# Tokens sorted by their pair of chosen experts, through HBM, in place of all eight experts for every token

## The chip, the cores and the metric

The kernel runs on one core of one Trainium2 chip. The metric is the device time of one execution in microseconds (us); less is better. Work is issued to TensorE (PE; its weight loads are shown apart as PEld), VectorE (DVE), ScalarE (ACT), GpSimd (POOL) and SyncE (SP), each of which runs its own instructions strictly in order; semaphores tie them together. SPq in a row is SP's queue, which only issues DMAs.

## The reference, cut to what matters

`x` is 32 images of 64 channels and 32x32 places, that is 32,768 tokens of 64 features. Three layers follow each other, each added to its input: a gated convolution of 1x1 kernels, a linear attention with its own small two-layer network, and the layer that the change touches, a mixture of 8 experts:

```python
logits = xf @ gate_w + gate_b
probs = jax.nn.softmax(logits, axis=-1)
top2_vals, top2_idx = jax.lax.top_k(probs, 2)
cw = jnp.zeros((N, Ee), dtype=xf.dtype).at[jnp.arange(N)[:, None], top2_idx].add(top2_vals)

def step(acc, params):
    w1, bb1, w2, bb2, we = params
    h = jax.nn.gelu(xf @ w1 + bb1, approximate=False)
    y = h @ w2 + bb2
    return (acc + we[:, None] * y, None)
out, _ = jax.lax.scan(step, jnp.zeros_like(xf), (W1, b1, W2, b2, cw.T))
```

D is 64, the hidden width 128, E is 8. `cw` is zero for the six experts that a token did not choose, so only two of the eight terms count. `xf` is the layer-normed token (mean 0 over its 64 features). Everything is float32.

## The kernel before, in words

The 32 images are taken in pairs (64 channels of two images fill the 128 partitions), two pairs at a time: `GROUPS` = 8 groups of `G` = 2 slots, a slot being 128 x 1024 (`T`) values, worked on in halves of `CH` = 512 columns. One group is 4,096 tokens.

**Dense work** of a group is a chain of small stages (a PE matmul, an ACT or DVE pass over its result, the next matmul): `channel_stats` to `conv_out` (the convolution), `centre_1` to `features_1` (a layer norm), `query` to `message` (the attention), then three layer norms of the form `variance_k`, `rstd_k`, `spread_k`, `norm_k` with `hidden_0`, `hidden_1`, `hidden_out` and `centre_4` between them. The last norm leaves the experts' input in `XF`. Then the **router** (`gates` to `gate_rows`): logits, softmax and the two largest on DVE, and the 8 weights of each token, transposed by PE (L830) and copied by DVE (L1343).

**Expert work** before: the router's rows go to HBM (`gates_hbm`, L524) and come back spread over the partitions as `CWB` (L533). A group has `US` = 32 units, one for each slot, expert and half. A unit is `first_layer` (L847: 2 matmuls of 64 rows x 128 columns of weights with 512 columns of data, one for each image of the pair, in two halves of the array's rows), `gelu` on ACT (L992, 128 x 1024), `second_layer` (L861: 2 matmuls in two halves of its columns), `combine` on DVE (L1355: add the bias, multiply by the token's weight for this expert) and `add_up` on POOL (L1044: into the sum `XB`). PE writes a float32 matmul as two records, so 2 matmuls are shown as x4.

**Order.** Every engine's program is written out from one table, `SCHEDULE`: in a turn, the dense stages of group `a` stand in a fixed order, and between them stand the steps of the experts of groups `b` and `c` (the earlier ones): letters for PE, counts for ACT and DVE. From the entry `first_unit` on they belong to group a-1, ahead of it to what is left of group a-2. `OPENING` is a table of its own for the start, in which group 0's dense work runs with group 1's convolution beside it, before any expert. The last group's experts have nothing beside them; they use more buffers then (`last_group`, `FREE`), so that PE runs two units ahead.

SP issues every DMA, in the program's order: the loads of `x` (L515), the router's rows out and back, and the stores of the result (`store`, L550).

## Time and profile before

| | |
|---|---|
| median of 3 runs | 1174.67 us (1172.91 to 1174.70) |
| span of the profiled execution, first to last instruction | 1171.7 us |
| PE busy | 1058.5 us, 90% of the span |
| DVE, ACT, POOL busy | 740.2, 641.8, 361.7 us |
| HBM read, written | 78.12 MB, 9.44 MB |
| instructions recorded | 16,823 |

The profiled execution's own time is its span and a few us around it: the runs' median lies 3.0 us over that span. Read from the table that PE is what is busy nearly all the time and that every other engine has a third of its time or more free. "Busy" is the union of an engine's records, so matmuls that overlap count once. The span falls into an opening, six repeats of one period, and an end; the windows below are cut there, at the starts of the router's logits (L815).

### The profile page before, as it was taken

The page shows a single profiled execution, that of the slowest core. Times are in us where ns is not written, and L with a number is a line of the kernel's source. Part 1 is how long each engine was busy: PE and PEld are TensorE (multiplying, and loading weights), DVE is VectorE, ACT ScalarE, POOL GpSimd, SP SyncE. Part 2 cuts the span into 40 slices and gives each one's busy share as a digit, 9 for nine tenths or more (in the row PEclk, how much of TensorE's full clock was granted, in tenths as well). Part 3 has the DMA queues.
Part 4 walks back from the last instruction along what each step waited for, and adds up shares of the span by engine and source line. Part 5 has one row for each costly group of instructions (what it writes and reads, how often), then busy time and mean ns, then how long its engine had stood idle before and what let it go on. Part 6 is the DMA issues. An engine that isn't in the chain of part 4 may idle for free.

```text
span 1171.7 us, 16823 instructions
## 1 busy us (share of the span) xinstructions
PE 1058.5 (90%) x6646; PEld 442.3 (38%) x6646; DVE 740.2 (63%) x1529; ACT 641.8 (55%) x866; POOL 361.7 (31%) x280
## 2 busy tenths in 40 slices
PE   4798589979999899988999899998999989998898
PEld 1453244323533245332453235432453324532232
DVE  5744745686647875587664966468764886556344
ACT  3345355654566556664556546556556555665454
POOL 0000031333323333333232333133332342324465
PEclk9989889999999999999999999999999999999999
DMA  5000086007700284005810068000850039200760
GB/s 157 6 1 1 1 179 149 3 22 173 169 1 19 54 189 104 1 19 112 185 50 1 19 149 198 1 19 19 194 134 1 18 69 201 42 1 19 179 145 23
DMA packets 15597, 88.62 MB, mean 76 GB/s; under 512 B 3488, under 2 KB 6816, under 8 KB 11424
## 3 DMA queue, kind: packets, MB, share of 16 engines
q1 hardware_dynamic: 15520, 87.57, 32.3%
q8 instruction: 52, 0.85, 0.3%
q14 instruction: 25, 0.20, 0.1%
HBM read 78.12 MB, written 9.44 MB: 75 GB/s over the span
## 4 chain that ended last, share of the span: by engine, by line
PE 74%; DVE 12%; ACT 9%; issue 3%; DMA 1%; DVEq 0%; POOL 0%; POOLq 0%; SPq 0%
PE HP L847 15%; PE HP L861 14%; ACT H L992 5%; PE R L646 5%; PE R L621 4%; PE R L610 4%; PE R L699 3%; PE R L717 2%; PE R L708 2%; PE R L786 2%; PE R L795 2%; PE R L788 2%; PE R L861 2%; PE R L675 2%; DVE TM L1355 2%
## 5 line engine op out<-in xcount | busy, mean ns | idle before, releaser
L1044 POOL TENSOR_TENSOR XB<-TM,XB 128x512 f32<-128x512 f32 x254 | 323.0, 1286 | 658.5 <-DVE TM L1355 658.5
L992 ACT ACTIVATE H<-HP,W 128x1024 f32<-128x1024 f32 x224 | 243.0, 1116 | 205.7 <-PE HP L847 205.1
L1355 DVE SCALAR_TENSOR_TENSOR TM<-HP,B2S,CWB 128x512 f32<-128x512 f32 x224 | 163.2, 742 | 207.1 <-PE HP L861 196.3
L847 PE MATMUL HP<-XF,W1E 64*128 64x512 f32 x1024 | 269.9, 630 | 19.3 <-DVE TM L1355 18.5
L861 PE MATMUL HP<-H,W 128*64 128x512 f32 x896 | 233.1, 616 | 18.0 <-ACT H L992 18.0
L847 PEld LDWEIGHTS HP<-XF,W1E 64*128 64x128 f32 x1024 | 84.1, 187 | 143.9 <-DVE TM L1355 71.0
L861 PEld LDWEIGHTS HP<-H,W 128*64 128x64 f32 x896 | 48.5, 135 | 171.2 <-ACT H L992 116.3
L1156 DVE SCALAR_TENSOR_TENSOR BIG<-R,T 128x512 f32<-128x512 f32 x112 | 69.5, 681 | 20.9 <-PE R L610 20.8
L930 ACT ACTIVATE T<-R 128x512 f32<-128x512 f32 x96 | 57.4, 598 | 39.8 <-PE R L646 31.4
L958 ACT ACTIVATE T<-R,MINUS 128x512 f32<-128x512 f32 x64 | 41.4, 688 | 27.3 <-PE R L708 24.4
L1243 DVE SCALAR_TENSOR_TENSOR BIG<-T,R 128x512 f32<-128x512 f32 x64 | 41.8, 684 | 21.6 <-ACT T L958 21.6
L610 PE MATMUL R<-IM,REP 32*128 32x512 f32 x336 | 50.2, 482 | 5.1 <-ACT T L918 2.3
L621 PE MATMUL R<-BIG,W 128*64 128x512 f32 x224 | 53.0, 617 | 1.9 <-DVE BIG L1156 1.9
L975 ACT ACTIVATE BIG<-R,BH 128x512 f32<-128x512 f32 x64 | 40.5, 683 | 21.7 <-PE R L788 21.7
L1035 POOL TENSOR_TENSOR XB<-XN,X 128x1024 f32<-128x1024 f32 x14 | 33.2, 2396 | 54.9 <-ACT XN L953 54.9
L992 ACT ACTIVATE BIG<-HP,W 128x1024 f32<-128x1024 f32 x32 | 33.9, 1110 | 26.0 <-PE HP L847 26.0
L1355 DVE SCALAR_TENSOR_TENSOR TM<-R,B2S,CWB 128x512 f32<-128x512 f32 x32 | 24.0, 751 | 37.8 <-PE R L861 35.1
L924 ACT ACTIVATE T<-R,W 128x512 f32<-128x512 f32 x28 | 19.2, 687 | 45.5 <-PE R L621 45.5
L1163 DVE TENSOR_TENSOR X<-X,T 128x512 f32<-128x512 f32 x28 | 21.6, 773 | 32.4 <-ACT T L924 32.4
L1218 DVE SCALAR_TENSOR_TENSOR T<-R,T 128x512 f32<-128x512 f32 x64 | 40.4, 682 | 1.9 <-PE R L675 1.7
L918 ACT ACTIVATE T<-R 128x512 f32<-128x512 f32 x56 | 29.1, 602 | 21.4 <-PE R L610 21.3
L610 PEld LDWEIGHTS R<-IM,REP 32*128 32x128 f32 x336 | 21.7, 202 | 48.1 <-issue 19.6
(179 smaller groups left out, 1411.3 us busy)
## 6 DMA issues: line engine op xcount, KB each, us to landing
CWB<-gates_hbm SPq DMA_DIRECT2D x32, 1536.0 KB, 20.4
CWB<-gates_hbm SPq DMA_DIRECT2D x32, 512.0 KB, 6.6
out<-XB SPq DMA_DIRECT2D x15, 512.0 KB, 3.0
X<-x SPq DMA_DIRECT2D x14, 512.0 KB, 3.8
XF<-x SPq DMA_DIRECT2D x2, 512.0 KB, 6.1
gates_hbm<-RT SPq DMA_DIRECT2D x16, 64.0 KB, 1.6
W<-wpack SPq DMA_DIRECT2D x1, 968.0 KB, 4.9
W1E<-w1e SPq DMA_DIRECT2D x1, 512.0 KB, 7.4
```

The source lines that it names most:

```text
L610: last = mm(Ra[s][:, half(c)], REP[rows, n, :], IM[rows, s, part, :], start=(part == 0), stop=(part == 1))
L621: last = mm(Ra[s][img(k), half(c)], w("ow")[:, C * h:C * h + C], BIGa[:, s, 2 * k + h, half(c)], start=(h == 0), stop=(h == 1))
L646: return mm(R[s][:, half(c)], weights, src[:, s, half(c)], start=True, stop=True)
L847: last = mm(HP[u % BATCH][:, half(k)], W1E[img(k), e, :], XF[img(k), 1 - par, s, half(c)], start=True, stop=True)
L861: last = mm(sums_of(b, u)[img(k), :], w("w2e")[:, C * e:C * e + C], activated(b, u)[:, k, :], start=True, stop=True)
L930: f(T2[:, s, half(c)], R[s][:, half(c)], ACT.Square).then_inc(ln_sq[s], 1)
L958: f(T1[:, s, half(c)], R[s][:, half(c)], ACT.Exp, bias=MINUS[:, :]).then_inc(qk_exp[s], 1)
L992: f(activated(b, u).rearrange("p k t -> p (k t)"), HP[u % BATCH][:, :], ACT.Gelu, bias=col(B1E + e))\
L1044: nc.gpsimd.tensor_tensor(acc, TM[:, u % BATCH, :], acc, ALU.add).then_inc(acc_done, 1)
L1156: v.scalar_tensor_tensor(out=BIGa[:, s, 2 * k + h, half(c)], in0=Ra[s][:, half(c)], scalar=1.0, in1=T2a[:, s, half(c)], op0=ALU.add, op1=A ...
L1243: v.scalar_tensor_tensor(out=dst[s][:, half(c)], in0=T1[:, s, half(c)], scalar=1.0, in1=R[s][:, half(c)], op0=ALU.min, op1=ALU.max).then_i ...
L1355: v.scalar_tensor_tensor(out=TM[:, u % BATCH, :], in0=sums_of(b, u), scalar=B2S[:, e % 2, e // 2:e // 2 + 1], in1=CWB[:, s, e, half(c)], o ...
```

## The change

Each token's pair of chosen experts is one of 28 classes (`CLS`, the pairs i<j). After the router, the group's 4,096 tokens are **sorted by class** and every class is filled up to whole blocks of 64 places (`BLK`); that takes at most 92 blocks (`BLOCKS`), 5,888 places. Each block needs only its pair's weights. What is added, for each group:

- `tokens_4` ("K", 4 steps): PE transposes the 32 tiles of tokens in 16 transposes of 128x128 (L938), ACT copies them to `XFT`, one token to a row of 64 features and two shares (the weights of its two experts).
- `classes`, `shares`, `sort_1` to `sort_3`: DVE makes a one-hot of the class, PE counts with 32 tiny matmuls (L949) and adds ranks (L960 to L963), DVE makes the place of each token (`IDX`) and the class of each block (`OF_BLOCK`).
- `scatter` (POOL): 32 indirect DMAs of 128 rows of 264 bytes to `slots_hbm`.
- 12 units (`US`) of 8 blocks (the last has 4). In a unit SP loads the places twice side by side (`unit_input`), and for each block **reads the block's class from SBUF into a register** (`value_load`) and issues a DMA of 128 KB, this pair's weights, from `pairs_hbm` (`pair_weights`). PE transposes the places ("T", `unit_features`), ACT copies them adding 1.0, PE runs the first layer ("A"): for each block 4 matmuls of 64 rows x 64 columns with 64 columns of data; ACT does gelu; the second layer ("B") has 4 matmuls of 128 rows x 64 columns with 64 columns for each two blocks; DVE multiplies by the shares and adds the pair's two results; SP writes them to `y_hbm`.
- `gather` (POOL): 32 indirect DMAs of 128 rows of 256 bytes back to token order. `final` ("F", 4 steps): PE turns them back to features with matmuls and adds the experts' second biases (`B2J` times the router's rows); DVE adds that to the sum.

The first bias is folded into the weights once, at the start (the input has mean 0, so 1.0 added to it meets a bias spread over 64 rows). There, too, `pairs_hbm` is written (28 DMAs) and `slots_hbm` filled with zeros. `CWB`, `gates_hbm`, `combine`'s bias and POOL's adding up are gone, and with them the last group's special case.

A group now passes through four turns instead of three: dense; then router, sort, scatter and the first units; then the remaining units and the gather; then `final` and `store`.

```diff
-CH_UNITS = E * NCH
-US = G * CH_UNITS
+PAIRED = [(d, i) for d in range(1, E) for i in range(E - d)]
+CLS = len(PAIRED)
+TOK = G * 2 * TB
+BLK = 64
+BLOCKS = (TOK * P + CLS * (BLK - 1)) // BLK + 1
+UB = CH // BLK
+US = -(-BLOCKS // UB)
...
 SCHEDULE = [
-    ("channel_stats", "HH", 1, 0), ("gates", "", 1, 0), ("gate_tokens", "YY", 0, 0),
...
+    ("channel_stats", "KA"), ("gates", "K"), ("gate_tokens", "TB"), ("gate_exp", ""), ("group_stats", "K"),
...
+    ("numerator.0", ""), ("numerator.1", ""), ("first_unit", ""), ("attended.0", ""), ("attended.1", "T"),
...
+            for n in range(GROUPS + 3):
+                turn(group(n), group(n - 1), group(n - 2), group(n - 3), parts)
...
+                def unit_input(u):
+
+                    n = a * US + u
+                    sp.wait_ge(scat_done, 16 * TOK * (a + 1))
+                    rows = slots_hbm[a % 2][CH * u:CH * u + P * columns(u), :].rearrange("(d p) c -> p d c", p=P)
+                    sp.dma_start(SLT[:, n % 3, 0:columns(u), 0:C], rows[:, :, 0:C]).then_inc(slt_in[n % 3], 16)
+                    sp.dma_start(SLT[:, n % 3, 0:columns(u), C:C + ROW], rows).then_inc(slt_in[n % 3], 16)
+
+                def pair_weights(g, u):
+
+                    n = g * US + u
+                    sp.wait_ge(cls_done, g + 1)
+                    for q in range(blocks_of(u)):
+                        pair = nc.sync.value_load(OF_BLOCK[0:1, g % 2, u * UB + q:u * UB + q + 1], min_val=0, max_val=CLS - 1)
+                        sp.dma_start(WB[:, n % 3, q, :],
+                                     pairs_hbm[bass.ds(pair, 1), :, :].rearrange("o p c -> p (o c)")).then_inc(wb_in[n % 4], 16)
...
+                def after(u):
+
+                    n = a * US + u
+                    sp.wait_ge(comb_read, n + 1)
+                    g, ahead = divmod(n + 3, US)
+                    if g < GROUPS:
+                        pair_weights(g, ahead)
+                        if g == a:
+                            unit_input(ahead)
+                    sp.wait_ge(yo_done, n + 1)
+                    sp.dma_start(y_hbm[a % 2][CH * u:CH * u + P * columns(u), :].rearrange("(d p) c -> p d c", p=P),
+                                 YO[:, n % 2, 0:columns(u), :]).then_inc(y_out[n % 2], 16)
...
+                def first_layer(u):
+
+                    n = a * US + u
+                    pe.wait_ge(xt_copied, n + 1)
+                    pe.wait_ge(*unit_weights(n))
+                    free("L1")
+                    for q in range(blocks_of(u)):
+                        for r in range(2):
+                            for h in range(2):
+                                last = mm(L1[img(h), CH * r + BLK * q:CH * r + BLK * q + BLK], WB[img(r), n % 3, q, img(h)],
+                                          XT[img(r), n % 2, BLK * q:BLK * q + BLK], start=True, stop=True)
...
+                def second_layer(u):
...
+                    for d in range(columns(u)):
+                        for r in range(2):
+                            for h in range(2):
+                                q = 2 * d + h
+                                last = mm(YPS[img(h), d, r, :], H[:, n % 2, r, BLK * q:BLK * q + BLK],
+                                          WB[:, n % 3, q, HID + C * r:HID + C * r + C], start=True, stop=True)
...
+                def scatter():
+
+                    pool.wait_ge(idx_done, a + 1)
+                    pool.wait_ge(tok_copied, (a + 1) * len(PIECES))
...
+                    for t in range(TOK):
+                        nc.gpsimd.indirect_dma_start(out=slots_hbm[a % 2], in_=XFT[:, t, :], in_offset=None,
+                                                     out_offset=bass.IndirectOffsetOnAxis(ap=IDX[:, a % 2, t:t + 1], axis=0))\
+                            .then_inc(scat_done, 16)
+
+                def gather():
+
+                    for k in range(2):
+                        pool.wait_ge(y_out[k], 16 * (US // 2) * (a + 1))
...
+                    v.tensor_tensor(YT[:, there, :, :], YPS[:, there, :, :],
+                                    SLT[:, n % 3, there, P:P + 2].unsqueeze(3).broadcast_to([P, columns(u), 2, C]), ALU.mult)\
+                        .then_inc(comb_read, 1)
...
+                    v.tensor_tensor(YO[:, n % 2, there, :], YT[:, there, 0, :], YT[:, there, 1, :], ALU.add).then_inc(yo_done, 1)
```

How the instructions stand now, at two places. **SP, one turn**, before (the waits are in brackets; L550 stores, L533 spreads the router's rows, L515 loads `x`, L524 writes the router's rows):

```order
L550 DMA out<-XB 128x1024 [waits acc_done]
L533 DMA CWB<-gates_hbm 64x2048 [waits comb_done]
L533 DMA CWB<-gates_hbm 64x2048
L533 DMA CWB<-gates_hbm 64x6144 x2
L515 DMA X<-x 128x1024 [waits xs_done0]
L515 DMA X<-x 128x1024 [waits xs_done1]
L550 DMA out<-XB 128x1024 [waits acc_done]
L524 DMA gates_hbm<-RT 128x128 [waits cwt_done]
L524 DMA gates_hbm<-RT 128x128
```

and SP of the change, between two units (CWB is the tensor in which all the new buffers lie; L595 and L596 are `unit_input`, L628 writes a unit's result, L603 is the read of the class with its register instructions, L604 the DMA of its weights):

```order
L595 DMA CWB<-slots_hbm 128x4x64 [waits scat_done]
L596 DMA CWB<-slots_hbm 128x4x66
L628 DMA y_hbm<-CWB 128x4x64 [waits yo_done]
L603 TENSOR_LOAD OF_BLOCK [waits cls_done,comb_read]
L603 ISA x2
L604 ISA
L604 DMA CWB<-pairs_hbm 128x256
L603 TENSOR_LOAD OF_BLOCK
```

In a period SP had 14 DMAs; it now has 92 reads of a class with 276 register instructions and 92 DMAs of weights, beside 40 others.

**PE, from the spreading of the attention's denominator (L770, now L869) to the second norm's spreading (L675, now L774)**, before:

```order
L770 MATMUL R<-BIG,SPREAD 128x256 x8
L847 MATMUL HP<-XF,W1E 128x512 x2
L646 MATMUL R<-T,WMC 128x512 x4
L861 MATMUL HP<-H,W 64x512 x2
L662 MATMUL R<-T,LINES 32x128 x16
L847 MATMUL HP<-XF,W1E 128x512 x2
L861 MATMUL HP<-H,W 64x512 x4
L675 MATMUL R<-BIG,SPAN 128x128 x16
```

and in the change (L972 "T", L985 "A", L1000 "B"):

```order
L869 MATMUL R<-BIG,SPREAD 128x256 x8
L972 MATMUL HP<-W,CWB 128x128 x4
L745 MATMUL R<-T,WMC 128x512 x4
L985 MATMUL HP<-CWB 64x64 x32
L761 MATMUL R<-T,LINES 32x128 x16
L972 MATMUL HP<-W,CWB 128x128 x4
L1000 MATMUL HP<-CWB,H 64x64 x16
L774 MATMUL R<-BIG,SPAN 128x128 x16
```

The dense matmuls and their order are the same; between them stand 32 and 16 matmuls of 64 columns where there were 2 to 4 of 512.

## Rows read from the trace of the kernel before

**Rows 1.** The page: busy time of the engines, and the chain that ended last

```profile
PE 1058.5 (90%) x6646; PEld 442.3 (38%) x6646; DVE 740.2 (63%) x1529; ACT 641.8 (55%) x866; POOL 361.7 (31%) x280
...
PE 74%; DVE 12%; ACT 9%; issue 3%; DMA 1%; DVEq 0%; POOL 0%; POOLq 0%; SPq 0%
```

**Rows 2.** Windows: from:to, length, busy of PE, PEld, DVE, ACT, POOL, clock, DMA, GB/s

```profile
0.00:137.00 137.00, 101.37 (x696) 52.26 (x696) 80.58 (x196) 54.66 (x94) 6.19 (x12) 0.96 0.12 35
137.00:234.40 97.40, 81.91 (x579) 37.92 (x578) 55.41 (x122) 52.11 (x73) 24.90 (x18) 0.93 0.45 100
...
373.10:511.80 138.70, 130.21 (x834) 54.19 (x832) 93.54 (x192) 80.34 (x109) 45.95 (x35) 1.00 0.34 78
...
1066.60:1171.70 105.10, 94.42 (x392) 27.33 (x384) 45.95 (x73) 53.29 (x51) 57.94 (x46) 0.98 0.43 99
```

**Rows 3.** One period by line: L847, L861 (PE, PEld), L1355 (DVE), L992 (ACT), L1044 (POOL)

```profile
373.10:511.80 138.70, 34.20 (x132) 10.59 (x130) 1.00 0.34 78
...
373.10:511.80 138.70, 32.99 (x128) 6.94 (x128) 1.00 0.34 78
...
373.10:511.80 138.70, 23.24 (x32) 1.00 0.34 78
...
373.10:511.80 138.70, 37.37 (x35) 1.00 0.34 78
...
373.10:511.80 138.70, 41.31 (x33) 1.00 0.34 78
```

**Rows 4.** L815, the logits, from the second group on: durations, first and last start

```profile
L815 PE MATMUL R<-XF,GWZ x112: 376/379/403, 234.5 to 1066.8; 128*32 128x256 f32 x112
```

**Rows 5.** Timeline of PE: start, length, line, shape, records [idle before]

```profile
438.66 1.09 PE L641 MATMUL R<-W,BIG 128*128 128x128 f32 x8
439.68 1.13 PE L847 MATMUL HP<-XF,W1E 64*128 64x512 f32 x4
...
447.15 1.05 PE L708 MATMUL R<-W,XN 128*128 128x128 f32 x8
448.04 0.38 PE L681 MATMUL R<-ONE 128*128 128x512 bf16 x1
...
469.64 1.08 PE L662 MATMUL R<-T,LINES 128*32 128x128 f32 x32
470.65 1.13 PE L847 MATMUL HP<-XF,W1E 64*128 64x512 f32 x4
```

**Rows 6.** SP's queue: two issues at the start; all issues of L533 (ns, min/median/max)

```profile
2.12 0.43 SPq L467 DMA_DIRECT2D BIG<-reps  x1
2.60 0.43 SPq L468 DMA_DIRECT2D BIG<-reps  x1
...
L533 SPq DMA_DIRECT2D CWB<-gates_hbm x64: 444/597/779, 151.8 to 1110.0; - x64
```

**Rows 7.** DMA: the hardware queue; issues with KB of each and us to landing

```profile
q1 hardware_dynamic: 15520, 87.57, 32.3%
...
gates_hbm<-RT SPq DMA_DIRECT2D x16, 64.0 KB, 1.6
```

**Rows 8.** Groups of instructions: busy us, mean ns of one | idle before

```profile
L1044 POOL TENSOR_TENSOR XB<-TM,XB 128x512 f32<-128x512 f32 x254 | 323.0, 1286 | 658.5 <-DVE TM L1355 658.5
...
L1035 POOL TENSOR_TENSOR XB<-XN,X 128x1024 f32<-128x1024 f32 x14 | 33.2, 2396 | 54.9 <-ACT XN L953 54.9
...
L1210 DVE TENSOR_TENSOR BIG<-R,SM 128x512 f32<-128x512 f32 x32 | 20.5, 683 | 0.2
...
L1327 DVE TENSOR_TENSOR RT<-RT 128x256 f32<-128x256 f32 x8 | 3.4, 426 | 0.3
```

**Rows 9.** Timeline of PE: the router's wait in the opening

```profile
138.71 0.44 PE L822 MATMUL HP<-W,BIG 128*128 128x128 f32 x2 [0.66 <-ACT BIG L981]
148.25 0.69 PE L830 MATMUL HP<-W,RT 128*128 128x128 f32 x2 [9.11 <-DVE RT L1333]
```

More of the change, by code:

```diff
@@ L552, in parts @@
-                return {**slotwise("features_1", next_input), "gate_rows": gate_weights,
-                        "weights_1": last_weights, "finish_0": lambda: store(0), "finish_1": lambda: store(1)}, lambda step, u: None
-            turns(parts, DVE_STEPS, apart=1)
+                        sp.wait_ge(pair_out, 16 * 4 * (E - 1))
+                        for u in range(3):
+                            pair_weights(a, u)
+                    for u in range(3):
+                        unit_input(u)
@@ new lines, in sort_3 @@
+                def sort_3():
+                    pe.wait_ge(d_done, 2 * (a + 1))
+                    for some, there in RANK_PARTS:
+                        mm(L1[:, there], BEFORE[:, :], MH[:, some, :].rearrange("p t k -> p (t k)"), start=True, stop=False)
+                        mm(L1[:, there], UNIT_ONE[0:CLS, :].broadcast_to([CLS, P]), RANKS[0:CLS, some.start * CLS:some.stop * CLS],
+                           start=False, stop=True)
+                    mm(TABLE, CLSID[0:CLS, :], OWNER[0:CLS, :], start=True, stop=True).then_inc(rank_ps, 1)
+                    last_read["L1"] = (cls_done, a + 1)
@@ L863, in second_layer @@
-                    last.then_inc(y_ps, 1)
-                def expert(step, u):
-                    if step == FIRST:
-                        if u < BATCH or not last_group(b):
-                            first_layer(u)
-                        return
-                    if last_group(b) and u % BATCH == 0:
-                        for ahead in range(u + BATCH, min(u + 2 * BATCH, US)):
-                            first_layer(ahead)
-                    second_layer(u)
+                    n = a * US + u
@@ new lines, in second_layer, with final @@
+                    last.then_inc(y_ps, 1)
+                def final(i):
+                    s, blocks, _ = tiles(i)
+                    if a == 0 and i == 0:
+                        pe.wait_ge(b_in, 16 * 2 * TB)
+                    pe.wait_ge(gath_done, 16 * TOK * (a + 1))
+                    free("XP")
+                    for k, j in enumerate(blocks):
+                        t = 2 * (s * TB + j)
+                        mm(XP[:, P * k:P * k + P], YG[:, t:t + 2, :].rearrange("p k c -> p (k c)"), w("ident"), start=(k == 0), stop=False)
+                    for k, j in enumerate(blocks):
+                        rows = img(j * NCH // TB)
+                        last = mm(XP[:, P * k:P * k + P], B2J[rows, k, :], CWR[rows, a % 3, s, :], start=False, stop=(j == blocks[-1]))
+                    last.then_inc(fin_ps, 1)
+                    last_read["XP"] = (fin_added, a * len(PIECES) + i + 1)
@@ L1054, in _ @@
+                return {**slotwise("features_1", residual), "sort_3": scatter, "gather": gather}, {}
+            turns(parts)
         @block.vector
@@ L1387, in parts @@
                     "choose_1": choose_1, "choose_2": choose_2, "gate_rows": gate_rows,
-                }, expert
-            turns(parts, DVE_STEPS)
+                    "classes": classes, "shares": shares, "sort_1": sort_1, "sort_2": sort_2, "sort_3": sort_3,
+                }, {"F": final, "B": combine}
+            turns(parts)
 def kernel(**inputs):
```

535 lines of the change are left out of this document (338 added, 197 removed), and 38 rows, old and new, of tables (OPENING, SCHEDULE).

## The prediction

> **What bounds it now.** I read the page first: PE is busy 90% of the span, and the chain that ended last is 74% PE [rows 1]. Then windows cut at the router's logits. The span is an opening of 137.0 us, a turn of 97.4, six periods, and an end of 105.1 [rows 2]; logits start at 234.5 and, six groups later, at 1066.8 [rows 4], so a period is 832.3 / 6 = 138.7 us. In it PE is busy 130.2 us at a clock of 1.00 (2.4 GHz), DVE 93.5, ACT 80.3, POOL 46.0, the DMA engines 34% [rows 2]. PE bounds it, and its idle time is 8.5 us. 34.2 + 33.0 = 67.2 us of PE's time are the experts [rows 3], the dense work is the other 63.0. The reader is to see two things: the six periods are 71% of the time, and in the end PE is still busy 94.4 of 105.1 us, since there the experts run at PE's pace.
>
> The sum goes: opening + turn + 6 periods + end, each priced anew.
>
> **The period, by PE.** Removed: 67.2 us. Added:
> - Small matmuls: 92 blocks x 4 in the first layer and 46 x 4 in the second are 552, two records each: 1,104. The nearest row is L662, where 32 records of 128 columns in quarters of the array go by in 470.65 - 469.64 = 1.01 us, 31.6 ns each [rows 5]. So 34.9 us. Bounds: below, four quadrants at once with 64 columns, half of L662's columns, 16 ns and 17 us; above, a full-width record as in L641 (1.02 us / 8 = 128 ns for 128 columns [rows 5]), halved for 64 columns, 64 ns and 71 us. I stay at L662, the only row with short records and part of the array.
> - Transposes: 46 of the units and 16 of the tokens at 128 ns: 7.9 us.
> - `final`: 32 matmuls of 128 columns as L708, (448.04 - 447.15) / 4 = 0.22 us [rows 5]: 7.1 us.
> - The sort: 32 tiny matmuls at L662's pace 1.0 us, and the rank and table matmuls, some 1,700 columns or 13 times 128, at L708's 0.22: 3.9 us in all.
>
> That is 53.8 us in place of 67.2: **PE gains 13 us a period, not the three quarters of the experts' work that the arithmetic drops**, because 552 matmuls of 64 columns cost by their number. With the 8.5 us of idle time the period by PE is 63.0 + 53.8 + 8.5 = 125.3 us.
>
> The Trainium skill (TensorE: Matmul & The Clock Gate, section "Wait — 56ns, not 53.3ns?") says that matmuls never start closer than about 25 ns however short; the 31.6 ns of the row respect that floor. At it, the 1,104 records would take 27.6 us and the period by PE would be 118.0; the row at 31.6 ns is what I use.
>
> **The period, by SP.** SP had 14 issues a period and idled; it now has 92 times a register read, three register instructions and a DMA issue, and 40 other DMAs. A plain issue takes 0.43 us and the next follows 0.05 us after it [rows 6]; L533's take 0.60. No row shows a register read. Bounds: below, the 0.05 us of a step that is not listed; above, 1.6 us, which is a whole small transfer from issue to landing [rows 7], since a read has its way there and back in common with one. I take 0.60, what the dearer plain issue L533 takes, as it is a trip without descriptors. A block is then 0.60 + 3 x 0.05 + 0.45 = 1.20 us, and a period 92 x 1.20 + 40 x 0.50 = 130.4 us. At the bounds: 80 and 222 us.
>
> The Trainium skill (DMA: Bandwidth & Descriptors, "Latency and other measured facts") gives about 600 ns as a register load's floor, and its rules warn that transfers under 64 KB are mostly overhead. A floor of 0.60 would take the cheap half of my bounds away and make a faster kernel less likely.
>
> So SP and PE lie within 5 us of each other, and PE must wait for weights where SP is late: **132 us** for the period, 6.7 less than before.
>
> **The period, other engines.** DVE loses L1355's 23.2 us [rows 3] and gains 12 x (0.68 + 0.43) = 13.3 for the products and sums [rows 8], some 3 for `final`, 13 for classes, shares and sorting: 100 us of 132, hidden but closer. ACT loses 37.4 and gains about 23. POOL loses 41.3 and gains 64 indirect DMAs. No row shows one: below is SP's 0.43, above L1035's 2.40, the longest POOL instruction; I take 1.3, L1044's 1.29 [rows 8], since both write 128 partitions from POOL: 83 us, hidden. The scatter takes 42 us between `sort_3` and the first "T", which are some 44 us apart: its cover is just enough. DMA: 78 GB/s x 138.7 us = 10.8 MB become 12.1 (weights) + 4.6 (places and results) + 2.1 (scatter, gather) + 2.1 = 20.9 MB; q1 moved 87.57 MB in 32.3% of the span, 231 GB/s [rows 7], so 90 us at that rate. Hidden, if 1 KB pieces go as fast.
>
> **Opening and turn.** Before, PE waited 9.1 us for the router in the opening [rows 9]. Group 0's sort now follows with nothing beside it: three round trips of PE and DVE, 12 us in which PE's dense work of group 1 stands behind the sort's matmuls. Then the scatter, 42 us, and only then the first "T"; the dense stages up to there cover some 25. So +29 us: 137 + 126 = 263. The tables, `pairs_hbm` and the zeros are written beside the opening, at nothing; without that cover they'd cost a few us.
>
> **The end.** Before 105.1 us. After the last logits 8 units of group 6 are left, then 12 of group 7, with no dense work beside them. PE needs some 4 us a unit; SP needs 8 x 1.20 + 3 x 0.50 = 11.1. Three units' weights are loaded ahead, so SP's pace holds for 8 + 9 = 17 units: 189 us. To that, 18 us for the first and the last of them to go through, 44 for the last gather, of which every one of 32 DMAs is on the path, 8 for `final` and the store: **259 us, 154 more than before**. What was a PE-bound end becomes an end bound by SP and by POOL.
>
> **Sum.** 263 + 6 x 132 + 259 = 1314 us of span, 142 more than 1171.7. The median of the runs is 3 us over the span: **1317 us**, 12% slower. As a formula: 263 + 6 x period + 17 x unit + 70.
>
> **Rivals.**
> - *Cheap register reads and matmuls that overlap (faster).* If a block costs SP 0.80 us (a read of 0.20), SP's period is 94 us and a unit 7.9. With small matmuls at 20 ns the period by PE is 112.5. Then 255 + 675 + 134 + 65 = 1129 span, 1132 us. The point from which it decides: the period below 117 with a block below 0.85 us. For it: PE's idle time is small, so what PE saves shows. Against it: L662 is dear though its columns are few. Both must hold, so 0.24.
> - *Both partly so (the same).* Period 118 and block 0.80: 255 + 708 + 134 + 70 = 1167 span, 1170 us. 0.04.
> - *Dear register reads.* At 1.6 us a block is 2.2: period 222, unit 19.1: 270 + 1332 + 325 + 75 = about 2000 us. At 1.0 us: 1.6, 167, 14.3: 263 + 1002 + 243 + 70 = 1578. Nothing in the trace speaks against it but L533. 0.12 for 1578 and up.
> - *Indirect DMAs dear.* At L1035's 2.4 us, POOL has 64 x 2.4 + 5 = 159 us a period, and scatter and gather are 77 us each: 298 + 954 + 189 + 105 = 1546, with 3 around it 1549 us. 0.08. The Trainium skill (SBUF — State Buffer, section "SBUF: two separate sides") says that GpSimd cannot write its DMA descriptors while DVE copies in its fast mode, which would be one way into this case; no row here shows it.
> - *DMA engines as the bound.* If 1 KB and 256 B pieces go at half of 231 GB/s, 20.9 MB take 181 us a period: 263 + 1086 + 259 = 1608. Against it: the register reads space the transfers. 0.04.
> - That it doesn't do what it says: I see no such way; the 92 blocks are computed whether full or not.
>
> **Chances and range.** The forecast, with its bounds (period 122 to 145, unit 10 to 12.5: 1235 to 1420), has 0.48. Of the middle case's 0.04, half lies within 0.2% (about what a measurement of this kernel can tell from no change) and a quarter on either side. So faster 0.25, the same 0.02, slower 0.73. The range leaves out the dear reads and the slow DMA engines, 0.16, and the fastest end of the cheap case: 1120 to 1570.
>
> **What would show it.** In the profile after, I look for: PE's busy time per period near 117 and its small records 30 ns apart; SP's queue solid with loads and issues, a block every 1.2 us; PE's longest waits at the first layer, for weights (`CWB` from `pairs_hbm`); a period of 132; DVE near 100 and POOL's 64 DMAs near 83 us; an end of some 260 us. The prediction is wrong if a block on SP takes under 0.85 us, or if scatter or gather DMAs, and not the weights, are what PE waits for.

## The result, and the profile after

The changed kernel takes **1512.7 us** (median of 4 runs, 1509.9 to 1519.6) where the one before takes 1174.7: a ratio of 1.289, 95% interval [1.285, 1.292]. It is slower, as forecast, and by 338 us, not by 142. The profiled execution took 1511.5 us, its span is 1509.7. Some kernels below have executions of two kinds, some per cent apart, the longer ones at a lower granted clock: the ratios compare the shorter ones, and the profiled executions of e5 and e6 (1406.4 and 1377.3 us) are of the longer kind.

The page of the changed kernel, busy time of the engines, the clock in 40 slices and the DMA queues (against [rows 1, 7]):

```profile
PE 1049.6 (70%) x14783; PEld 709.8 (47%) x14798; DVE 735.9 (49%) x1702; ACT 531.7 (35%) x832; POOL 543.9 (36%) x545
...
PEclk9899679969797979788989798988889895657755
...
q1 hardware_dynamic: 272400, 159.30, 40.1%
q0 software_dynamic: 16384, 17.07, 4.8%
```

PE has as much busy time as before, in a span 29% longer, and its clock, at or near full speed nearly everywhere before, swings in every period.

Windows of the changed kernel at the same places of the program as [rows 2]: opening, turn, one of the six periods, end (from:to, length, busy of PE, PEld, DVE, ACT, POOL, clock, DMA share, GB/s):

```profile
0.00:151.10 151.10, 114.49 (x726) 61.56 (x730) 82.91 (x203) 54.70 (x94) 7.68 (x19) 0.95 0.29 84
151.10:277.80 126.70, 73.43 (x974) 46.39 (x974) 60.08 (x140) 41.12 (x68) 36.01 (x34) 0.78 0.28 71
595.30:754.10 158.80, 125.62 (x1859) 85.31 (x1865) 92.39 (x214) 66.64 (x105) 67.40 (x66) 0.87 0.52 134
1230.40:1509.70 279.30, 127.76 (x2093) 107.30 (x2085) 45.85 (x100) 34.99 (x46) 92.35 (x96) 0.63 0.44 114
```

The logits (L914 now, against [rows 4]):

```profile
L914 PE MATMUL R<-XF,GWZ x112: 379/379/403, 277.8 to 1230.6; 128*32 128x256 f32 x112
```

So a period is (1230.6 - 277.8) / 6 = 158.8 us. By the parts of my sum: opening and turn 277.8 (I said 263), periods 953 (792), end 279 (259). Of the 196 us that I missed in the span, **161 lie in the periods**: each is 26.8 us longer than forecast. In one, PE is idle for 33.2 us, where I kept the 8.5 of before.

What PE waits for in that period, by line (us in total, times, longest):

```profile
PE HP L972 <- DMA CWB<-slots_hbm: 16.7, 4, 10.2
PE R L774 <- DVE BIG L1399: 3.5, 3, 1.2
PE HP L938 <- DVE XF L1411: 2.9, 2, 1.4
PE R L745 <- DVE XB L1424: 2.5, 2, 1.6
```

The largest wait is at the transposes of "T", for the **places** of a unit, not at the first layer for weights. Over the six periods it comes to 105.0 us in 21 times, 17.5 a period. SP's queue around the longest of them (start, length, issues):

```profile
685.35 8.38 SPq L604 DMA_DIRECT2D CWB<-pairs_hbm  x8
693.78 0.43 SPq L628 DMA_DIRECT2D y_hbm<-CWB  x1
695.03 8.02 SPq L604 DMA_DIRECT2D CWB<-pairs_hbm  x8
703.10 0.43 SPq L628 DMA_DIRECT2D y_hbm<-CWB  x1
703.58 0.47 SPq L595 DMA_DIRECT2D CWB<-slots_hbm  x1
```

and PE there:

```profile
706.80 1.12 PE L972 MATMUL HP<-W,CWB 128*128 128x128 f32 x4 [10.25 <-DMA CWB<-slots_hbm]
```

The places of the new group's first unit stand in line behind 16 tiles of weights, those of the second and third unit, which are not needed yet. SP is not solid: in this period it waits too.

```profile
SPq L603 <- DVE CWB L1593: 28.3, 4, 11.6
```

Those 28.3 us are waits for a free weight buffer (VectorE's L1593 is the step that ends a unit's use of it). SP works in bursts: idle, then some 9 us for a unit, with what is urgent at the end of the burst. What one block costs it (ns, min/median/max):

```profile
L603 SPq TENSOR_LOAD <-OF_BLOCK x736: 262/268/901, 183.7 to 1433.5; - x184
L603 SPq FUSED_REGOPS  x736: 152/152/188, 184.3 to 1433.8; - x184
...
L604 SPq DMA_DIRECT2D CWB<-pairs_hbm x736: 337/338/1090, 184.8 to 1434.2; - x184
```

Eight blocks take about 8.9 us with the read ahead of the first, 1.12 each.

### The profile page after: what moved, and what is told of

The parts are those of the page before. It is cut to its first block and busy times, and to the rows that moved or that the text cites. A ratio compares the mean times of both kernels' runs of the same rounds, so it can differ in the third digit from the quotient of the medians.

```text
span 1509.7 us, 38760 instructions
## 1 busy us (share of the span) xinstructions
PE 1049.6 (70%) x14783; PEld 709.8 (47%) x14798; DVE 735.9 (49%) x1702; ACT 531.7 (35%) x832; POOL 543.9 (36%) x545
## 5 line engine op out<-in xcount | busy, mean ns | idle before, releaser
L1212 POOL DMA_INDIRECT slots_hbm<-CWB,IDX x256 | 254.7, 995 | 488.4 <-DVE IDX L1579 412.8
L1223 POOL DMA_INDIRECT CWB<-y_hbm,IDX x256 | 248.7, 972 | 293.8 <-issue 198.5
L972 PE MATMUL HP<-W,CWB 128*128 128x128 f32 x368 | 76.5, 340 | 240.6 <-DMA CWB<-slots_hbm 224.7
L1593 DVE TENSOR_TENSOR CWB<-HP,CWB 128x512 f32<-128x512 f32 x96 | 63.8, 664 | 258.5 <-PE HP L1000 258.5
L1154 ACT ACTIVATE H<-HP 128x1024 f32<-128x1024 f32 x96 | 94.9, 989 | 248.7 <-PE HP L985 222.4
L972 PEld LDWEIGHTS HP<-W,CWB 128*128 128x128 f32 x368 | 48.4, 169 | 277.1 <-DMA CWB<-slots_hbm 244.3
L1000 PE MATMUL HP<-CWB,H 128*64 128x64 f32 x2944 | 130.7, 254 | 6.6 <-ACT H L1154 6.5
L1000 PEld LDWEIGHTS HP<-CWB,H 128*64 128x64 f32 x2944 | 117.0, 165 | 31.3 <-issue 19.0
L985 PE MATMUL HP<-CWB 64*64 64x64 f32 x5888 | 126.8, 244 | 5.1 <-DVE OF_BLOCK L1574 4.4
L985 PEld LDWEIGHTS HP<-CWB 64*64 64x64 f32 x5888 | 112.8, 156 | 32.1 <-issue 26.6
L1013 PE MATMUL HP<-W,CWB 128*128 128x128 f32 x256 | 47.8, 344 | 49.0 <-DMA CWB<-y_hbm,IDX 44.7
L1013 PEld LDWEIGHTS HP<-W,CWB 128*128 128x128 f32 x256 | 40.7, 242 | 59.4 <-DMA CWB<-y_hbm,IDX 44.8
```

The costliest lines, as they stand in the source:

```text
L972: last = nc.tensor.transpose(XP[:, P * d:P * d + P], SLT[:, n % 3, d, 0:P], w("ident"))
L985: last = mm(L1[img(h), CH * r + BLK * q:CH * r + BLK * q + BLK], WB[img(r), n % 3, q, img(h)], XT[img(r), n % 2, BLK * q:BLK * q + BLK], s ...
L1000: last = mm(YPS[img(h), d, r, :], H[:, n % 2, r, BLK * q:BLK * q + BLK], WB[:, n % 3, q, HID + C * r:HID + C * r + C], start=True, stop=True)
L1013: mm(XP[:, P * k:P * k + P], YG[:, t:t + 2, :].rearrange("p k c -> p (k c)"), w("ident"), start=(k == 0), stop=False)
L1154: f(H[:, n % 2, :, some], L1.rearrange("p (r t) -> p r t", r=2)[:, :, some], ACT.Gelu).then_inc(gelu_done, 1)
L1212: nc.gpsimd.indirect_dma_start(out=slots_hbm[a % 2], in_=XFT[:, t, :], in_offset=None, out_offset=bass.IndirectOffsetOnAxis(ap=IDX[:, a % ...
```

## The experiments

All kernels in one table; periods and ends are cut at the logits as above, from the profiled execution, whose mean clock stands in the last column. A row's median is that of all its runs.

| kernel | median us | ratio to before | period | end | clock |
|---|---|---|---|---|---|
| before | 1174.7 | 1 | 138.7 | 105 | 0.985 |
| the change | 1512.7 | 1.289 [1.285, 1.292] | 158.8 | 279 | 0.83 |
| e1 pairs fixed | 1392.8 | 1.184 [1.179, 1.190] | 147.5 | 229 | 0.844 |
| e4 places first | 1448.8 | 1.234 [1.229, 1.238] | 149.6 | 281 | 0.824 |
| e5 both | 1381.4 | 1.175 [1.172, 1.178] | 146.2 | 253 | 0.831 |
| e3 weights once | 1342.5 | 1.141 [1.135, 1.146] | 139.4 | 221 | 0.895 |
| e13 fixed, small tiles | 1388.8 | 1.183 [1.178, 1.188] | 147.8 | 223 | 0.846 |
| e14 once, reads kept | 1397.3 | 1.191 [1.187, 1.195] | 148.1 | 225 | 0.847 |
| e2 first within a group | 1496.5 | 1.275 [1.271, 1.278] | 157.7 | 274 | 0.817 |
| e9 first and shared | 1445.8 | 1.231 [1.226, 1.237] | 149.1 | 264 | 0.839 |
| e8 plain DMAs | 1444.3 | 1.230 [1.222, 1.238] | 156.0 | 242 | 0.842 |
| e6 once and first | 1370.7 | (1345 to 1377) | 144.8 | 229 | 0.844 |
| e7 units thin | 1406.9 | 1.197 [1.193, 1.201] | 148.4 | 227 | 0.755 |
| e10 thin and busy | 1432.0 | 1.221 [1.213, 1.228] | 149.1 | 236 | 0.872 |
| e11 first and busy | 1526.7 | 1.299 [1.294, 1.303] | 157.8 | 280 | 0.89 |
| e12 before, half | 1112.3 | 0.947 [0.943, 0.950] | 131.7 | 84 | 0.913 |
| e15 before, eighth | 1163.1 | 0.990 [0.987, 0.993] | 140.2 | 85 | 0.741 |

### SP: the order of its queue, or how much it does

**e1**, in `pair_weights`:

```diff
-  pair = nc.sync.value_load(OF_BLOCK[0:1, g % 2, u * UB + q:u * UB + q + 1], min_val=0, max_val=CLS - 1)
+  pair = (u * UB + q) % CLS
```

> The register read of each block's pair (L603) is replaced by a pair fixed in the program, so 92 reads per group and their register arithmetic are gone, while the same 92 tiles of the same size are still loaded, from fixed places of the table (the output is then not the reference's). A block's time on SP should fall from 1.12 us to about 0.55. Theory A, the order of SP's queue (places of a unit stand behind 8 to 24 tiles): these runs of tiles get half as long, so part of the waits goes, period 158.8 -> 145 to 152, total 1400 to 1465. Theory B, the reads make SP the bound: period falls to what TensorE needs, 125 to 132, total 1270 to 1320. Theory C, the dense chain's own latency sets the period: total 1490 to 1512.

**e4**, in SP's `after`; `begin` loads places for the first group alone:

```diff
   if g < GROUPS:
+      unit_input(g, ahead)
       pair_weights(g, ahead)
-      if g == a:
-          unit_input(ahead)
```

> Nothing is left out; only the order on SP changes: the places of unit n+3 are issued before its 8 tiles, and across the group boundary too, so the first three units of a group no longer stand behind 16 to 24 tiles of SP's work. Reads and tiles stay 92. Theory A: the waits of the transposes (L972) nearly vanish, TensorE's clock rises with its idle gone, period 158.8 -> 132 to 142, end 279 -> about 255, total 1320 to 1390. Theory B (SP's throughput, register reads): same work on SP, so no more than 1% off, 1495 to 1512. Theory C (dense chain's latency): periods within 2 us of 158.8, only the end gains 10 to 20 us, 1480 to 1500.

**e5** is both.

> Both edits together: pairs fixed in the program and places first (output not the reference's, for the fixed pairs). Theory A: nearly all of the gain is that of places first, the fixed pairs add under 15 us: 1310 to 1375. Theory B: as with fixed pairs alone, 1270 to 1320. Theory C: 1475 to 1500.

**e3**, in `pair_weights`, with the waits for weights moved to the first three units' semaphores:

```diff
   n = g * US + u
+  if n >= 3:
+      return
```

> The tiles of weights are loaded for the first three units alone and kept, all later units compute with these (output not the reference's): SP and the DMA engines are relieved of 713 of 736 reads and tiles (some 72 MB), the places' order stays as it is, but with nothing in front of them. Theory A: as places first, period 130 to 140, total 1310 to 1380. Theory B: the same or better than fixed pairs, 1260 to 1320. Theory C: 1475 to 1500. If DMA contention of the tiles is what makes places late, this gains clearly more (over 30 us) than places first with fixed pairs.

Measured: e1 took 11.3 us off a period, e4 9.2, and no tiles at all 19.4. Theory A's ranges hold e1's period, and e3's period and total; they miss e4 and e5, and the other two theories miss all four. e5's 12.6 us come from an execution of 1406.4 us, 25 us above its median, so the totals are the better measure of it: e1 gains 119.9 us, e4 63.9, both together 131.3, no tiles at all 170.2. With places first the longest waits for them shrink, but a new one comes up at the first layer: in e4 as a whole (L984 is the first layer there, L971 the transposes),

```profile
PE HP L984 <- issue: 75.5, 17, 7.4
PE HP L971 <- DMA CWB<-slots_hbm: 46.3, 7, 27.8
```

where the change had 224.7 us in 36 waits for places. "issue" names no releaser there. L984 stands behind the wait for the unit's weights, and what was issued earlier on SP went to the places, so I read it as late weights. It matters where these waits lie: in e4's six periods there is no wait for places left (105.0 us in the change) and 9.0 us at L984; 66.5 us at L984 lie in the end, which did not get shorter (281 us). Order and amount are thus two handles on one lateness: a burst of SP that is too long for the gap it must fit in. They don't add up (119.9 + 63.9 against 131.3), and together they don't reach what goes when the tiles go.

Three kernels split this further. **e13** is e1 with tiles of 128x16 after the third unit (`some = slice(0, 4 * BLK if n < 3 else 16)`), **e14** is e3 with the register reads kept, **e2** is e4 with `if g == a:` in front of the early `unit_input`, so that a group's first three units keep the change's order.

> Fixed pairs, and each tile after the first three units' is 128x16 in place of 128x256 (4.6 MB in place of 73; the rest of the held weights is old, so the output is not the reference's): SP issues as many DMAs as with fixed pairs at full size, whose period is 147.5 and total 1393; with no tiles at all (weights once) it was 139.4 and 1342. If the bytes of the tiles on the DMA engines make things late: period 139 to 142, total 1335 to 1360. If SP's issues in order do: period 145 to 148, total 1375 to 1395.

> Weights once, but SP still reads each block's pair into a register (92 reads a period, 0.5 to 0.6 us each), and issues no tile for it (output not the reference's). Weights once alone: period 139.4, total 1342. If the reads' time on SP counts as much as the issues' (both hold the queue for about half of 1.12 us): period 145 to 149, total 1370 to 1400, like fixed pairs. If only the transfers count: within 2 us of 139.4, total 1340 to 1355.

> Nothing is left out. Places are issued before the tiles only within a group; at a group's start the order is the changed kernel's, so SP never stands at the next group's scatter with tiles and stores behind it, as it could for 13.5 us with places first everywhere (period 149.6, end 280.6, total 1449). If that new wait ate the gain: end 260 to 268, total 1400 to 1440. If SP's 11 us a unit set the end whatever the order, end 275 to 282, and with the first units' places late again a period of 152 to 157: total 1460 to 1495.

Measured periods: issues without reads and nearly without bytes 147.8; reads without issues or bytes 148.1; with neither 139.4. **The bytes count for nothing** (147.5 with all of them, 147.8 with a sixteenth, though the DMA share falls from 0.52 to 0.31), which takes away the reading that e3's forecast allowed, contention of the tiles on the DMA engines. Both kernels came out where the forecasts put them if SP's commands count, and e2 a little over the second of its cases. Reads alone are 8.7 us a period over e3 and issues alone 8.4, but not all of that is their price. The waits for places that come back are 3.9 and 3.3 us a period; the rest is PE's busy time at a lower clock (means of 122.2 and 122.8 us over the six periods, 117.3 in e3), and e6 below has as much of that with neither reads nor issues. And e2's 157.7 shows where order matters: within a group the order brings 1.1 of e4's 9.2 us, the rest comes from the three first units, whose places stand behind the next group's tiles.

**e9** is e4 and, besides, gives the last two tiles of each unit from the fourth on to ScalarE's queue, behind the GELU of the unit two before:

```diff
+  act.wait_ge(comb_read, n)
+  for q in range(blocks_of(v) - 2, blocks_of(v)):
+      pair = nc.scalar.value_load(OF_BLOCK[...], min_val=0, max_val=CLS - 1)
+      act.dma_start(WB[:, m % 3, q, :], pairs_hbm[bass.ds(pair, 1), :, :]...)
```

> Nothing is left out. Places first as before, and from the fourth unit of a group on the last two tiles of each unit (20 of 92 with those of the half unit) are read and issued on ScalarE's queue, behind the unit's GELU. SP has 18 to 20 tiles less, some 21 us a period; ScalarE has as much more, beside 67 us of its own. Theory D: waits for weights shrink from places first, period 149.6 -> 143 to 147, total 1400 to 1430. If ScalarE's waits and reads hold the dense chain up as much as they relieve SP, 1440 to 1470.

It moves the time of e4 by nothing that can be told apart: a period of 149.1 against 149.6, medians of 1445.8 against 1448.8. That is the total of the forecast's second case. The end is 16 us shorter in the profiled runs, but these are e4's slowest and e9's fastest. No routed version that computes everything was faster than these two.

### GpSimd: scatter and gather

**e8**: one plain DMA of the same bytes in place of each 32 indirect ones.

```diff
-  for t in range(TOK):
-      nc.gpsimd.indirect_dma_start(out=slots_hbm[a % 2], in_=XFT[:, t, :], ...)
+  nc.gpsimd.dma_start(slots_hbm[a % 2][0:P * TOK, :].rearrange("(t p) c -> p t c", p=P), XFT[:, :, :])
```

> The changed kernel with the 32 indirect DMAs of each scatter and of each gather replaced by one plain DMA of the same bytes, at fixed places (tokens go to no block of their own, output not the reference's). Theory D: scatter and gather are hidden in the periods (SP's tiles and their order stand as they were), so periods stay at 156 to 159 us; only the end loses the gather of about 41 us less what the plain DMA takes (5 to 10), and 0 to 15 at the last group's start: total 1455 to 1480. A rival by which GpSimd's 1.27 us a DMA (81 us a period) makes places late all along: period 135 to 145, total 1330 to 1400.

Measured: a period loses 2.8 us, the turn's end comes 14.5 us earlier (263.3 against 277.8), the end loses 37. The periods are as theory D has them. So the 64 indirect DMAs are hidden in the periods but for a little, and stand on the path once at each end of the program. It came out faster than I expected, by 11 us.

### TensorE: the idle time that I took as fixed, and the clock

> Weights loaded for the first three units alone, and places first besides (output not the reference's). What weights once left of late places was 27.8 us at a group's start in the turn and in the end. Theory D, the one that the first four runs leave: a period is 139.4 us without any lateness of SP (TensorE's busy 117.6 and 22 of idle that the dense layers' own chain leaves), and SP's bursts add 19.4. Then nothing is left for the order to bring: period 138 to 140, total 1325 to 1345. Theory A' (places are still late by their place in the queue): period 132 to 136, total 1290 to 1315.

**e6** (e3 and e4 together) ran from 1345 to 1377 us, at mean clocks of 0.875 and 0.844, the clock following no edit. One period of e3, and one of e6:

```profile
555.40:694.80 139.40, 117.89 (x1839) 79.57 (x1838) 89.83 (x204) 65.69 (x103) 67.89 (x66) 0.95 0.27 65
...
567.00:711.80 144.80, 124.63 (x1833) 85.50 (x1837) 90.35 (x209) 64.97 (x102) 67.00 (x66) 0.88 0.27 63
```

The instructions are the same, tiles are late in neither, and PE is idle for about as long (22.1 and 21.9 us a period over the six). The 5.4 us between the two periods are PE's busy time, at 0.95 and at 0.88 of the full clock. The forecast of e6 was missed by this, and it settles nothing on the order. It also says how far to trust the table: e3's profiled run is one of its two fastest (1336.2, of 1334.7 to 1362.0), so what a difference to e3's period says of a cause can be wrong by some 5 us.

**e7** is e6 with the loops over a unit's blocks cut to the first: `for q in range(1)` and `for d in range(1)`.

> As weights once with places first, and of each unit's 64 + 32 small matmuls only 4 + 4 are done (most of the experts' products are left out, output not the reference's). TensorE's busy time falls by about 11 units x (60 x 17 ns + 28 x 34 ns) = 22 us a period. If TensorE's work sets the period of 139.4, it falls by all of it, to about 117, total near 1160. If the chain through the dense layers sets it with latencies that units only partly cover (theory D), it falls by a third to a half of that, to 128 to 133, total 1230 to 1275.

Neither of the two forecasts: with some 22 us of work less in a period, the kernel got **slower** than e3 (1407 against 1342) and than every run of e6. The clock is the thing that changed, from 0.95 in e3's periods to about 0.8:

```profile
573.00:721.50 148.50, 117.95 (x961) 71.39 (x961) 94.02 (x221) 68.42 (x108) 67.18 (x66) 0.82 0.26 60
```

PE's busy time is that of e3, 117.9 us, with 878 matmul records less.

**e10** and **e11** put useless matmuls back: 6 and 5 a unit in e7; in e4 4 a unit, and 24 more at the first unit of a group and at every unit of the first group. To make room for them, PE's wait for the free PSUM bank also moved ahead of its wait for weights (in e11 for places too). e10 took 1410 to 1441 us, where e7 took 1395 to 1408.

```diff
...
+  for _ in range(times):
+      for k in range(bank.shape[1] // CH):
+          mm(bank[:, half(k)], BEFORE[:, :], BEFORE[:, :].unsqueeze(1).broadcast_to([P, 4, P]), start=True, stop=True)
```

> As units thin (all but 8 of a unit's 96 small matmuls left out, weights once, places first), with matmuls that nobody needs in their stead: 6 of 128x512 in bf16 in front of each unit's first layer and 5 in front of its second, some 2.3 us a unit at full clock, about what the small matmuls took (output not the reference's). Theory E, the clock: leaving work out took the steady clock from 0.95 to about 0.75 and made a period of 139.4 one of 148.4; useless work gives the clock back, and with it the time: period 137 to 141, clock over 0.93, total 1320 to 1350. If the clock has another cause (the tiles, the chip's day), the added work can only add: period 149 to 165, total 1410 to 1530.

> Nothing is left out; places first, and useless matmuls of 128x512 in bf16 on TensorE: 4 in front of each unit's wait for its weights (0.85 us) and 24 (5.1 us) in front of the wait for places of each unit of the first group and of the first unit of the others. They add some 12 x 0.85 + 5 = 15 us of work to a period. Theory E, the clock: a part of them lies in idle time and the clock rises from 0.82 towards 0.95, so that the time does not rise and may fall: period 143 to 150, total 1410 to 1450. If the clock does not follow TensorE's own activity: periods 155 to 165, total 1490 to 1560.

Both theories lose here. The clock did come back (0.95 in one of e10's periods, 0.89 in the next; e11 0.94 to 0.97), but the period did not: 149.1 and 157.8, which are the times of the cases in which the clock does not follow the added work, as it did. The matmuls filled PE's idle time and brought no earlier end (e10: PE busy 132 us a period for 118, idle 17 for 30). In e11 PE is busy for 138 us a period where e4 has 125, and idle for 18 where e4 has 25; that its matmuls stood in front of work that was ready is my reading of this, and no run shows it. Filling in idle time by an instruction that can't be skipped when the engine is not idle bought nothing in either place.

The cleanest test needs no routing. **e12** and **e15** are the kernel before with narrower expert matmuls, all else equal:

```diff
-  last = mm(HP[u % BATCH][:, half(k)], W1E[img(k), e, :], XF[img(k), 1 - par, s, half(c)],
+  last = mm(HP[u % BATCH][:, half(k)][:, 0:2 * P], W1E[img(k), e, :], XF[img(k), 1 - par, s, half(c)][:, 0:2 * P],
```

and the same at L861; 64 columns in e15.

> The kernel before, with the experts' matmuls over 256 of each 512 columns in both layers (half of their products is left out, output not the reference's); all else as it was, so TensorE has some 31 us less of work in a period of 138.7, and nothing is routed. By my sum (TensorE's busy and 8.5 us of idle) a period falls to 108 to 115, total 960 to 1000, or to what VectorE and the dense chain's latency allow. Theory E with the latency of the dense chain: the clock falls below 0.9, and a period stays at 125 to 140, total 1080 to 1175.

> The kernel before, with the experts' matmuls over 64 of each 512 columns (seven eighths of their products left out, output not the reference's): TensorE's work in a period would fall from 130 to some 75 us at full clock. Half of the columns left 131.7 of 138.7. Theory E (the dense chain has a length of its own, and TensorE's clock falls as work is taken out, so the dense matmuls on the chain get slower): period 128 to 145, clock under 0.8, total 1090 to 1190. A pure chain of latencies with no part for the clock: 115 to 126, total 990 to 1070.

The periods and totals of both are those of theory E, and not those of my sum (108 to 115 for e12); e12's clock, 0.90 to 0.96 in its periods, stayed a little over the 0.9 that it named. One period of e12, below it the largest waits in it, and the same two lines in a period of the kernel before:

```profile
498.10:629.80 131.70, 112.15 (x822) 57.49 (x824) 90.86 (x183) 78.76 (x106) 45.86 (x34) 0.91 0.35 80
```

```profile
PE HP L861 <- ACT H L992: 8.8, 12, 1.5
PE HP L847 <- DVE TM L1355: 2.4, 3, 1.4
```

```profile
PE HP L847 <- DVE TM L1355: 3.0, 4, 1.5
PE HP L861 <- ACT H L992: 2.3, 7, 0.6
```

One period of e15, whole, then L847 and L861 alone:

```profile
516.60:656.80 140.20, 112.42 (x836) 66.73 (x842) 94.26 (x193) 80.27 (x108) 45.79 (x34) 0.73 0.34 80
...
516.60:656.80 140.20, 17.22 (x128) 0.73 0.34 80
...
516.60:656.80 140.20, 11.97 (x128) 0.73 0.34 80
```

| kernel before with | period | PE idle | experts on PE | dense on PE | clock |
|---|---|---|---|---|---|
| 512 columns | 138.7 | 8.5 | 67.2 | 63.0 | 1.00 |
| 256 (e12) | 131.7 | 19.5 | 45.3 | 66.9 | 0.91 |
| 64 (e15) | 140.2 | 27.8 | 29.2 | 83.2 | 0.73 |

The reader is to see three things. Taking 21.9 us of expert work out of a period brings 7.0; taking 38.0 out brings **nothing, 1.5 us more** than before. The idle time grows as work goes, since PE's matmuls were what covered the passes of VectorE and ScalarE between them, those of the dense layers and those of the units themselves: of the 11 us more in e12, 6 are at the units' own matmuls (11.2 us for 5.3, mostly the second layer waiting for its GELU), the rest at the dense layers and the router. And the dense column grows: the same dense instructions take 63.0, 66.9 and 83.2 us, as the granted clock falls from full speed to a mean between the two levels of 2.4 and 1.2 GHz. Read from e15 to e12, three eighths of the expert columns *added* make a period 8.5 us shorter and the kernel 51 us faster.

A piece of e15's PE timeline shows it at work:

```profile
543.49 0.69 PE L847 MATMUL HP<-XF,W1E 64*128 64x64 f32 x4 [1.97 <-DVE TM L1355]
544.12 1.23 PE L610 MATMUL R<-IM,REP 32*128 32x512 f32 x8
545.28 0.70 PE L861 MATMUL HP<-H,W 128*64 128x64 f32 x8
546.51 2.20 PE L610 MATMUL R<-IM,REP 32*128 32x512 f32 x8 [0.53 <-ACT T L918]
```

Eight records of L610 take 1.23 us in one place and 2.20 a moment later, after idle time and narrow matmuls. The Trainium skill (TensorE: Matmul & The Clock Gate, section "HAM oscillation — how this bites in real kernels") describes waits for DMA that let the clock fall, so that the next stretch starts at half speed; the trace agrees, and shows that waits for VectorE and ScalarE, and thinner work, go with it too: none of PE's waits in this period of e15 is for a DMA.

## Why the prediction was right or wrong

- **Direction: right, and in part by luck.** It is slower, and the chance of 0.73 was on that side; 1512.7 lies in the wide range of 1120 to 1570, but above the forecast's own 1235 to 1420. That three quarters of the arithmetic buys PE little held, and so did the end that SP and POOL bound: it takes 174 us more than before (forecast 154; e1 takes 50 us off it, e8 37), opening and turn 43 more (29). But I had the six periods 40 us shorter than before in all, and they are 121 us longer. More than a third of the slowdown thus comes from the place where I expected a gain.
- **SP's price: nearly right.** A block takes 1.12 us, forecast 1.20; a unit in the end, where SP does not wait, 10.5 to 11.3, forecast 11.1. But the read is 0.27 us, not 0.60, and the register arithmetic and the gaps make up for it; the sum was right, its parts were not. SP is occupied for 158.8 - 31 = 128 us of a period, forecast 130.4.
- **PE's busy time: 125.6 us, forecast 116.8.** The small matmuls take 16.2 + 15.8 = 32.0 us (34.9), transposes 12.3 (7.9), `final` 11.1 (7.1), the sort 4.3 (3.9); dense work 66.0 (63.0). In e3, whose clock is 0.95, transposes are 9.8, small matmuls 28.8 and the whole is 117.9, so the count was right and the excess goes with the clock.
- **The step that failed: "With the 8.5 us of idle time the period by PE is 63.0 + 53.8 + 8.5 = 125.3 us", and with it the 132.** I took PE's idle time for a constant, and that SP and PE "lie within 5 us of each other" for a wait of 2 us. Idle time is 33.2 us, 16.7 of it for places. The runs part it so: without the reads and issues of tiles 19.4 us of period go (e3), 11.7 of them idle time and 7.7 busy time at a lower clock (14.4 and 5.0 as means of the six periods); how much of the busy time is the edit's doing and how much the execution's own clock is not shown, as e6 differs from e3 by 5.4. What stays is 21.5 us of idle time, 13 over mine: 12.7 at the dense layers' own waits, 5.1 at a wait that is new with the change, and 3.9 at the units, the sort and the tokens. The new one is L972, where "T" waits for VectorE's last step of `final`, since both use the PSUM bank `XP`; it stands at the head of e3's waits in that period.

```profile
PE HP L972 <- DVE XB L1605: 5.1, 2, 5.0
PE R L774 <- DVE BIG L1399: 3.6, 3, 1.3
```

  In the kernel before, the dense layers and the router took 3.1 us of idle time a period, and e12 shows how both kinds grow when work is taken out. Two engines at 80% each, working in bursts for one another through three buffers, are not one engine at 80%.
- **What PE waits for.** I said weights at the first layer. It waits for places at the transposes (224.7 us in all), as the line "scatter or gather DMAs, and not the weights" warned. Yet it is neither of these DMAs: it is their plain successor behind tiles on SP (e2, e4). The indirect DMAs of scatter and gather are together worth 2.8 us a period (e8).
- **POOL: right.** An indirect DMA takes 0.97 and 0.96 us and the next starts 1.27 after it, forecast 1.3. **DVE** 92.4, forecast 100. **DMA engines**: hidden, as forecast; e13 shows it.
- **Opening: 151.1, forecast 137.** "The tables, `pairs_hbm` and the zeros are written beside the opening, at nothing" failed: the 16 matmuls that make the tables' weights with the bias folded in (L659, L660; 32 records) stand on PE for 11.6 us. The turn is 126.7, forecast 126.
- **The end: 279, forecast 259.** The miss is not in the gather (41 us from its first issue to `final`, forecast 44), but at most 8 us in the units and 15 in `final` and the store, 22.7 for my 8. PE had sat idle for 44.7 us, and all four steps of this `final` run at half speed:

```profile
1487.00 2.07 PE L1013 MATMUL HP<-W,CWB 128*128 128x128 f32 x8 [44.69 <-DMA CWB<-y_hbm,IDX]
1489.00 2.07 PE L1016 MATMUL HP<-CWB,B2J 64*128 64x128 f32 x8
```

  In a period of the same trace the same eight take about half:

```profile
616.07 1.16 PE L1013 MATMUL HP<-W,CWB 128*128 128x128 f32 x8
```

- **The rivals.** Cheap reads did come true in the read itself (0.27 us), and were worth nothing, since the block's other steps were dearer. None of my rivals had either of the mechanisms that mattered: a burst of SP puts the next unit's places behind tiles, and work taken out of an engine that fills gaps makes the gaps visible, and its clock fall.

**What stays open.** How the 13 us of idle time in e3 divide between the chain's latencies and the slower matmuls on it was not tried; no run here holds the clock without costing PE time. A PSUM bank of its own for `final` was not tried either. Why e6 ran at another clock than e3, and differently from run to run, is not known: they ran on different chips, on which the kernel before takes the same time (1174.4 and 1175.4), but e3's four runs on one chip are spread over 27 us too.

## What to carry to other kernels

Before taking work off an engine, ask what that work was hiding: cut it by half without doing anything else (as in e12) and see what the period does; here that one run would have shown that a period gives back a third of the busy time taken out (7.0 of 21.9 us), and a second, at seven eighths, that it gives back nothing, before any routing is paid for. In a queue that issues in order, put what is needed next ahead of what is needed in three steps, and count register reads as commands of that queue: bytes cost nothing here (e13), reads did (e1 gains 8%). A table of busy times does not add up to a period when engines serve each other in bursts through few buffers.

## What the hardware showed that I had not expected

- A register read from SBUF on SP takes 0.27 us, of a block's 1.12. The Trainium skill (DMA: Bandwidth & Descriptors, "Latency and other measured facts") gives a floor of about 600 ns; the measurement decides, and with the register arithmetic (0.15 us in its longest step) and the gaps behind it the whole still costs more than half a block: in e1, without them, eight tiles are issued in as little as 3.7 us.
- Records of short fp32 matmuls on quarters of the array go by at 17 ns each, on halves at 34: in two groups of e3's timeline, 64 and 32 records in 1.09 and 1.08 us by the starts of what follows. The Trainium skill (TensorE: Matmul & The Clock Gate, section "Wait — 56ns, not 53.3ns?") gives about 25 ns as the least distance of two starts; the 17 ns are below it if a record counts as a matmul, and above it if the two records of one float32 matmul count as one (34 ns), which no run here decides.

```profile
738.47 1.15 PE L1000 MATMUL HP<-CWB,H 128*64 128x64 f32 x32
739.55 1.39 PE L709 MATMUL R<-IM,REP 32*128 32x512 f32 x8
740.88 1.16 PE L985 MATMUL HP<-CWB 64*64 64x64 f32 x64
741.97 0.65 PE L720 MATMUL R<-BIG,W 128*64 128x512 f32 x2
```

- Leaving out seven eighths of the columns of the experts' matmuls from the kernel before, with no other change, saves 12 us of 1175, and leaving out half of them saves 62.
